# Tables' rows by partition, own semaphores and four buffers for the h rows, and a division moved to ScalarE, in a graph network on one Trainium2 core

## What is computed

```
L0: h = relu(x@W1 + b1) @ W2;  out = segment_sum(h[src]*norm, dst) + own term + b2
L1: out = gcn(relu(gcn(x, W1)), W2), gcn(h) = segment_sum(norm*h[src], dst) + own term
L2: z = leaky_relu(x) @ W;  e = leaky_relu(el[src] + er[dst]);  ex = exp(e - emax[dst])
    out = segment_sum(ex/denom[dst] * z[src], dst) + bias
L3: messages = relu([x[src], x[dst], edge] @ mW1 + mb1) @ mW2
    out = relu([x, segment_sum(messages, dst)] @ uW1 + ub1) @ uW2 + ub2
```

## Time and profile before

| | |
|---|---|
| median of 3 runs | 2941.12 us (2938.37 to 2942.83) |
| the profiled execution | 2938.16 us |
| its span, first to last instruction | 2936.4 us |
| busy share of the span: PE, DVE, ACT, POOL | 74%, 68%, 49%, 74% |
| mean granted TensorE clock | 0.848 of full speed |
| DMA packets | 624033, of them 536606 under 512 B; 338.13 MB |
| chain that ended last, by engine | POOL 57%, issue 19%, PE 9%, DVE 8%, DMA 3% |

### The profile page before, as it was taken

One profiled execution on the slowest core, in us unless ns is written; L12 is line 12 of the kernel. 1 busy time (PEld: TensorE's weight loads), 2 busy tenths in 40 slices (PEclk: granted clock), 3 DMA queues, 4 the chain that ended last, 5 costly groups with the idle time before them and its releaser, 6 DMA issues.

```text
span 2936.4 us, 39046 instructions
## 1 busy us (share of the span) xinstructions
PE 2171.1 (74%) x10332; PEld 1155.7 (39%) x10332; DVE 1984.6 (68%) x3848; ACT 1429.8 (49%) x2755; POOL 2169.0 (74%) x1666
## 2 busy tenths in 40 slices
PE   3998899968778757777687759998356576666665
PEld 1444444434445324444343434444155233333332
DVE  6665688858888747777599968998699343333332
ACT  2877677745444436665344437777222232223332
POOL 7888878778888268886788858888233688888887
PEclk9999999979898768888789979999555787777777
DMA  7998522224556455555344445555477322222221
GB/s 210 285 271 241 144 57 54 59 58 93 129 130 141 93 128 125 128 133 125 78 112 113 111 95 127 141 137 125 94 191 186 77 62 52 55 57 57 54 53 26
DMA packets 624033, 338.13 MB, mean 115 GB/s; under 512 B 536606, under 2 KB 585100, under 8 KB 623817
## 3 DMA queue, kind: packets, MB, share of 16 engines
q1 hardware_dynamic: 550217, 288.96, 39.1%
q0 software_dynamic: 73600, 46.68, 9.4%
HBM read 203.61 MB, written 130.80 MB: 114 GB/s over the span
## 4 chain that ended last, share of the span: by engine, by line
POOL 57%; issue 19%; PE 9%; DVE 8%; DMA 3%; SPq 1%; ACT 1%; DVEq 0%; POOLq 0%; ACTq 0%
POOL g_row L857 42%; POOL x_with_info L864 8%; POOL out_rows L864 8%; PE bank L1075 2%; PE bank L1098 1%; DVE rT L1685 1%; PE bank L984 1%; PE pair L1055 1%; DMA g_row<-t_x,gidx 1%; PE pair L984 1%; DMA g_row<-in_x,dst_i 1%; DVE x_r L1662 1%; DVE ss L1608 1%; PE pair L1066 0%; DVE w_r L2007 0%
## 5 line engine op out<-in xcount | busy, mean ns | idle before, releaser
L857 POOL DMA_INDIRECT g_row<-t_x,gidx x600 | 808.1, 1347 | 258.6 <-issue 217.3
L1281 ACT ACTIVATE hid<-pair,b_up 128x1000 f32<-128x1000 f32 x375 | 406.0, 1083 | 42.9 <-PE pair L1056 42.1
L1076 PE MATMUL bank<-hid,w_dn 128*64 128x500 f32 x750 | 420.8, 644 | 0.0
L1075 PE MATMUL bank<-hid,w_dn 128*64 128x500 f32 x750 | 420.7, 644 | 0.0
L1055 PE MATMUL pair<-xT,w_top 64*128 64x500 f32 x550 | 316.7, 657 | 15.5 <-ACT hid L1281 15.0
L857 POOL DMA_INDIRECT g_row<-x_with_info,src_i x200 | 275.3, 1377 | 63.8 <-issue 55.8
L1056 PE MATMUL pair<-xT,w_bot 64*128 64x500 f32 x550 | 317.5, 658 | 0.0
L857 POOL DMA_INDIRECT g_row<-t_h,gidx x200 | 261.5, 1307 | 75.7 <-issue 75.7
L857 POOL DMA_INDIRECT g_row<-in_x,dst_i x200 | 261.1, 1306 | 68.7 <-issue 68.1
L1262 ACT ACTIVATE xT<-bank 128x500 f32<-128x500 f32 x275 | 160.2, 583 | 295.3 <-DVE rT L1685 163.2
L864 POOL DMA_INDIRECT out_rows<-n_r,fidx x200 | 248.8, 1244 | 61.6 <-issue 60.3
(11 more groups left out here) (257 smaller groups left out, 5205.0 us busy)
## 6 DMA issues: line engine op xcount, KB each, us to landing
x_in<-in_x_cols SPq DMA_DIRECT2D x100, 250.0 KB
x_with_info<-wide SPq DMA_DIRECT2D x50, 476.0 KB
wide<-in_x SPq DMA_DIRECT2D x50, 448.0 KB
out_rows<-x_r SPq DMA_DIRECT2D x100, 224.0 KB
l_k<-keep_row SPq DMA_DIRECT2D x150, 125.0 KB
l_a<-t_x SPq DMA_DIRECT2D x150, 112.0 KB
l_k<-on_row SPq DMA_DIRECT2D x50, 250.0 KB
t_x<-x_r SPq DMA_DIRECT2D x100, 112.0 KB
```

The source lines that it names most:

```text
L857: return g.indirect_dma_start(out=to, out_offset=None, in_=table, in_offset=bass.IndirectOffsetOnAxis(ap=index[:, tile:tile + 1], axis=0), ...
L1075: T.matmul(run.down[0:D, 0:CH], w_dn[a.stage][:, 0:D], hid[a.b2][:, 0, :], start=True, stop=True)
L1076: T.matmul(run.down[D:128, 0:CH], w_dn[a.stage][:, 0:D], hid[a.b2][:, 1, :], start=True, stop=True)\
L1281: A.activation(hid[a.b2][:, :, :], run.up[a.b2][:, :, 0:CH], ACT.Relu, bias=b_up[:, a.stage:a.stage + 1]).then_inc(Cn["hid"], 1)
```

## The change

The rows of a table are stored by partition: chunk c, partition p, tile k is row c*500 + p*4 + k; iso block b, partition p, place j is row b*1000 + p*8 + j. The two iotas behind `gidx` follow. `in_pairs` is gone, and stores of iso rows go out in two pieces of 2 KB runs. The h2 rows get four buffers (two idle ones of the same size are taken in) and four semaphores of their own; the x2 stores get three. In G, v_r is made on ScalarE by four activations with the reciprocal as scale, at the head of ScalarE's slot; DVE's reciprocal waits for the v_r before. The diff, cut:

```diff
         def chunks(ap):
-            return ap.rearrange("(c k p) f -> c p k f", k=TC, p=R)
+            return ap.rearrange("(c p k) f -> c p k f", k=TC, p=R)
+
+        def chunk_pairs(ap):
+            return ap.rearrange("(b s p k) f -> b p s (k f)", s=2, k=TC, p=R)

         def blocks(ap):
-            return ap.rearrange("(b j p) f -> b p j f", j=TB, p=R)
+            return ap.rearrange("(b p j) f -> b p (j f)", j=TB, p=R)
...
-        h2_r = [b[0:R, :] for b in h2_r_all]
+        h2_r = [b[0:R, :] for b in h0_r_all + h2_r_all]
...
-                        for to, frm in in_pairs(blocks(t1_d[E:2 * E, :])[a.b], x1_r[a.r4]):
+                        for to, frm in in_two(blocks(t1_d[E:2 * E, :])[a.b], x1_r[a.r4][:, :]):
...
-                        for to, frm in in_pairs(blocks(t2_d[E:2 * E, :])[a.b], h2_r[a.b % 2]):
-                            sp.dma_start(to, frm).then_inc(s1_sem[a.b % 2], 16)
+                        for to, frm in in_two(blocks(t2_d[E:2 * E, :])[a.b], h2_r[a.b % 4][:, :]):
+                            sp.dma_start(to, frm).then_inc(h2_sem[a.b % 4], 16)
                         sp.wait_ge(Cn["rows"], normed(a))
-                        for to, frm in in_pairs(blocks(t3_d[E:2 * E, :])[a.b], x2_r[a.r3]):
-                            sp.dma_start(to, frm).then_inc(s1_sem[a.b % 2], 16)
+                        for to, frm in in_two(blocks(t3_d[E:2 * E, :])[a.b], x2_r[a.r3][:, :]):
+                            sp.dma_start(to, frm).then_inc(s1_sem[a.b % 3], 16)
...
-                for to, frm in in_two(blocks(t1_d[0:E, :])[b], n_view(a_rows[b % 2])):
+                for to, frm in in_two(chunk_pairs(t1_d[0:E, :])[b], a_rows[b % 2].rearrange("p (s c) -> p s c", s=2)):
...
-                        for to, frm in in_two(blocks(t4_d[E:2 * E, :])[b], n_view(third_out[b % 2])):
+                        for to, frm in in_two(blocks(t4_d[E:2 * E, :])[b], third_out[b % 2]):
...
-            g.iota(slot_id[:, :], pattern=[[R, NT]], base=1, channel_multiplier=1,
+            g.iota(slot_id[:, :], pattern=[[CH, NC], [1, TC]], base=1, channel_multiplier=TC,
...
-            g.iota(gbase[:, :], pattern=[[R, NT]], base=E, channel_multiplier=1,
+            g.iota(gbase[:, :], pattern=[[BLK, NI], [1, 2], [2, TC]], base=E, channel_multiplier=TB,
...
@@ ScalarE, slot_g @@
+                if c := at(2):
+                    k, q, h, p = c
+                    at_least(act, LE["rden"], k + 1)
+                    at_least(act, LE["t2"], k)
+                    for i in range(TC):
+                        part = A.activation(v_r[:, i * D:(i + 1) * D], AT[0:R, i * 128:i * 128 + D], ACT.Copy,
+                                            scale=lrden[:, i:i + 1])
+                    part.then_inc(LE["t1"].sem, 1)
...
-                        at_least(dve, iso_sem1[a.b % 2], 128 * (a.b // 2))
-                        V.tensor_tensor(h2_r[a.b % 2][:, :], run.rows[a.b2][0:R, :], x1_r[a.r4][:, :], ALU.subtract).then_inc(Cn["h2"], 1)
+                        at_least(dve, Cn[f"h2st{a.b % 4}"], 32 * (a.b // 4))
+                        V.tensor_tensor(h2_r[a.b % 4][:, :], run.rows[a.b2][0:R, :], x1_r[a.r4][:, :], ALU.subtract).then_inc(Cn["h2"], 1)
...
-                            par, times = iso_stored(a.s - 3)
-                            dve.wait_ge(iso_sem1[par], 128 * times)
+                            dve.wait_ge(iso_sem1[SEQ[a.s - 3].b % 3], 32 * (SEQ[a.s - 3].b // 3 + 1))
...
@@ DVE, slot_g @@
                     at_least(dve, LE["den"], k + 1)
+                    at_least(dve, LE["t1"], k)
                     V.reciprocal(lrden[:, :], lden[:, :]).then_inc(LE["rden"].sem, 1)
-                if c := at(2):
-                    k, q, h, p = c
-                    at_least(dve, LE["rden"], k + 1)
-                    at_least(dve, LE["t2"], k)
-                    V.tensor_tensor(v4(v_r[:, :]), AT65[:, :, 0:D], spread(lrden[:, :], TC), ALU.mult).then_inc(LE["t1"].sem, 1)
```

More of the change, by code:

```diff
@@ L310, in build @@
         Cn = sems("chain", "rowsT xT up hid dn res resT h2 h2b sq ssum std rstd"
-                           " rows y sq2 ssum2 std2 rstd2 rows2 info in0 in1 in2 out0 out1 dsq0 dsq1 dsq2 dsq3 scaled based base0 base1 s0st0 s0st1 s1st0 s1st1")
+                           " rows y sq2 ssum2 std2 rstd2 rows2 info in0 in1 in2 out0 out1 dsq0 dsq1 dsq2 dsq3 scaled based base0 base1 s0st0 s0st1 s1st0 s1st1 s1st2 h2st0 h2st1 h2st2 h2st3")
         ctx.enter_context(nc.allow_non_contiguous_dma(reason="bias columns and the chunks' neighbours, once"))
@@ L446, in third_steps @@
                     yield step, (k - at) // 2
[L448 to L452, removed]
         def in_two(to, frm):
@@ L601, in _ @@
             base_sem = [Cn["base0"], Cn["base1"]]
-            s0_sem, s1_sem = [Cn["s0st0"], Cn["s0st1"]], [Cn["s1st0"], Cn["s1st1"]]
+            s0_sem, s1_sem = [Cn["s0st0"], Cn["s0st1"]], [Cn[f"s1st{r}"] for r in range(3)]
+            h2_sem = [Cn[f"h2st{r}"] for r in range(4)]
             asked = [0]
@@ L632, in slot @@
                         sp.wait_ge(Cn["based"], a.b + 1)
-                        for to, frm in in_two(blocks(base0_d)[a.b], n_view(own_base[a.b % 2][:, :])):
+                        for to, frm in in_two(blocks(base0_d)[a.b], own_base[a.b % 2][:, :]):
                             sp.dma_start(to, frm).then_inc(base_sem[a.b % 2], 16)
@@ L664, in ld_a @@
                 at_least(sp, LA["t2"], b - 3)
-                for to, frm in in_two(n_view(a_base[b % 4]), blocks(base0_d)[b]):
+                for to, frm in in_two(a_base[b % 4], blocks(base0_d)[b]):
                     sp.dma_start(to, frm).then_inc(A_ld[b % 4].sem, 16)
@@ L739, in ld_third @@
             def ld_third(b):
-                for to, frm in in_two(n_view(third_in[b % 2]), blocks(t3_d[E:2 * E, :])[b]):
+                for to, frm in in_two(third_in[b % 2], blocks(t3_d[E:2 * E, :])[b]):
                     sp.dma_start(to, frm).then_inc(third_ld[b % 2], 16)
@@ L745, in third @@
                 if k < 0:
+                    for r in range(3):
+                        sp.wait_ge(s1_sem[r], 32 * len(range(r, NI, 3)))
                     for b in range(2):
-                        sp.wait_ge(s1_sem[b], 128 * len(range(b, NI, 2)))
                         ld_third(b)
@@ L928, in _ @@
             for r in range(2):
-                pool.wait_ge([Cn["s0st0"], Cn["s0st1"]][r], 64 * len(range(r, NI, 2)))
+                pool.wait_ge([Cn["s0st0"], Cn["s0st1"]][r], 32 * len(range(r, NI, 2)))
             all_stored(pool, A_st, NI)
             gather_level(t1_d, B_ga, LB["msg"])
-            for r in range(2):
-                pool.wait_ge([Cn["s1st0"], Cn["s1st1"]][r], 128 * len(range(r, NI, 2)))
+            for r in range(4):
+                pool.wait_ge(Cn[f"h2st{r}"], 32 * len(range(r, NI, 4)))
             all_stored(pool, B_st)
@@ L1595, in _ @@
             assert c[1] == PREP_ALL
-            iso_sem0, iso_sem1 = [Cn["s0st0"], Cn["s0st1"]], [Cn["s1st0"], Cn["s1st1"]]
+            iso_sem0, iso_sem1 = [Cn["s0st0"], Cn["s0st1"]], [Cn[f"s1st{r}"] for r in range(3)]
             def chain(run):
@@ L1609, in first @@
                     if a and a.stage == 0 and a.iso:
-                        at_least(dve, iso_sem0[a.b % 2], 64 * (a.b // 2))
+                        at_least(dve, iso_sem0[a.b % 2], 32 * (a.b // 2))
                         V.tensor_copy(info_r[:, a.b * TB:(a.b + 1) * TB, :], xs_rows[a.b % 4][:, :, D:XW]).then_inc(Cn["info"], 1)
                     if a and a.stage == 1 and a.iso:
-                        at_least(dve, iso_sem1[a.b % 2], 128 * (a.b // 2))
-                        V.tensor_tensor(h2_r[a.b % 2][:, :], run.rows[a.b2][0:R, :], x1_r[a.r4][:, :], ALU.subtract).then_inc(Cn["h2"], 1)
+                        at_least(dve, Cn[f"h2st{a.b % 4}"], 32 * (a.b // 4))
+                        V.tensor_tensor(h2_r[a.b % 4][:, :], run.rows[a.b2][0:R, :], x1_r[a.r4][:, :], ALU.subtract).then_inc(Cn["h2"], 1)
                         dve.wait_ge(Cn["h2"], a.b + 1)
-                        V.tensor_tensor(n_view(h2_r[a.b % 2][:, :]), n_view(h2_r[a.b % 2][:, :]), row_bias(1, TB),
+                        V.tensor_tensor(n_view(h2_r[a.b % 4][:, :]), n_view(h2_r[a.b % 4][:, :]), row_bias(1, TB),
                                         ALU.subtract).then_inc(Cn["h2b"], 1)
@@ L1653, in rest @@
                                 par, times = iso_stored(a.s - 4)
-                                dve.wait_ge(iso_sem0[par], 64 * times)
+                                dve.wait_ge(iso_sem0[par], 32 * times)
                         if a.stage == 1 and a.s >= 3 and SEQ[a.s - 3].iso:
-                            par, times = iso_stored(a.s - 3)
-                            dve.wait_ge(iso_sem1[par], 128 * times)
+                            dve.wait_ge(iso_sem1[SEQ[a.s - 3].b % 3], 32 * (SEQ[a.s - 3].b // 3 + 1))
                         if a.stage == 2:
@@ L1914, in _ @@
             for r in range(2):
```

(7 more changed lines are left out.)

## The result

The changed kernel took **2922.79 us** at the median of four runs (2918.18 to 2927.77); the kernel before, run beside it on the same chip, 2940.21 us (2938.37 to 2942.83). The ratio is 0.994 with a 95% interval of 0.9922 to 0.9959: faster by 0.6%. I had predicted 2943.6 us with a range of 2926 to 2959, and no change that can be told as the likeliest.

The account below looks back on a forecast made before the run. It took GpSimd's gathers and scatters as the bound in all stages but G, plus the waits between stages, and the AT loop in G. Sum -15.8 - 2.2 + 20.5 = +2.5 us on 2941.12: 2943.6 us, range 2926 to 2959.

Parts of the forecast that it names:

- no change that can be told: Whole kernel: the forecast itself, a time of 2935 to 2947 us; chance 0.42.
- Point 1: Tail of A: four h buffers and separate semaphores remove DVE's waits before the h row; 15.8 us gained.
- the two waits: Tail of A: DVE idle 8.59 and 8.15 us before the h row, 16.7 us, of which 15.8 stay won.
- The rivals in which the wait passes over to the x2 store, whole or for one turn: Tail of A: whole, 2959 us, chance 0.03; one turn, +8 us, 2951 us, chance 0.10.
- Point 2: Stage ends: fewer, longer store pieces shorten landings by 0.6 and 1.0 us, 0.6 for B, C, G; 2.2 us gained.
- Point 4: G: v_r as four ScalarE activations, 1.02 us, lengthens the AT loop's turn from 3.28 to 3.85 us; 20.5 us lost.
- The DVE rival: G: DVE is the bound, so moving v_r off it gains 17 us; 2906 us, chance 0.07.
- Point 3: Row order, iotas and loads in 256-byte runs: nothing on a path, GpSimd's gathers keep 1.27 us; no effect.

Follow-up runs that it names:

- buffers alone: Kernel before with only the four h buffers and separate semaphores; old row order, four-piece stores, v_r on DVE: 2923.43 us, ratio 0.9929.
- rows alone: Kernel before with only rows by partition and two-piece stores; two h buffers on shared semaphores, v_r on DVE: 2919.11 us, ratio 0.9924.
- v_r alone: Kernel before with only v_r moved from DVE to four ScalarE activations in G: 2955.91 us, ratio 1.0044.

## Why the prediction was wrong

**Point 1, the wait in A: right.** I took 15.8 us for the two waits; buffers alone take 14.2 to 15.0 from the gap. The x2 store did not come into the way, as I had argued from its landing. The rivals in which the wait passes over to the x2 store, whole or for one turn, are out.

**Point 2, the landings: about right in sum, too dear in each landing.** A's last store takes 2.80 us and not 2.85, where I expected 0.6 less; it is 2.85 to 2.96 us in the five profiles of the old order and 2.69 to 3.02 in the eight of the new one. The last store of the third pass takes 2.51 and not 2.99, where I expected 1.0 less; 2.89 to 3.02 us in the old order, 2.48 to 2.66 in the seven of the new one whose chain passes through it. The gaps gave 1 to 2 us in A (rows alone) and 1.8 at the mean from D to G: 3 to 4 us against 2.2. By the Trainium skill (DMA: Bandwidth & Descriptors, "Why small descriptors are slow (HBM only)") it would have been 27% of a landing at most; the two landings shrank by 2% and 16%, which stays below that bound.

**Point 4, v_r in G: right in its mechanism, a little too dear.** Four activations take 0.93 us, not 1.02: a turn is 3.76 us against my 3.85, and 49 turns of 0.09 us are the 4.5 us by which the sum was too high. I expected +20.5 us; the profiles show +16.0, and the comparisons of times +13 (v_r alone) and +16 to +20 (the change with and without it). The DVE rival, G faster by 17 us, is out while AT has one bank; with two, DVE is the nearest bound, and taking v_r off it shortens G by 7 us. The rule of the Trainium skill (ScalarE: Activation LUTs, "Rules for kernel authors") that multiplications belong on VectorE held for the kernel as changed; with two banks G was shorter by 7 us against the rule, in one profile of each, while the times overlap. By the same page ("What ACT_TABLE_LOAD costs") one activation would take 332 ns and four, overlapping, 1.05 us, an estimate from its fixed costs and its price per element; the trace has 315 ns for one (L1409, median) and 0.93 us for four, which is less.

**Point 3, the row order: this is the step that failed.** I wrote of the other order of rows "nothing on a path; GpSimd's gathers keep their 1.27 us", and that M stays as long as before. The median did stay. The mean did not: GpSimd's busy time in M fell by 11.2 us and M by 10.5, in all six profiles with the new order and M's code untouched, and in none with the old. What the runs show in its place is the meeting of GpSimd's transfers with DVE's scan over the messages: in the new order fewer transfers start early in it. With M at -10.5 in place of nothing, G at +16.0 and the rest as measured, the sum is -18.4 - 1.8 + 16.0 - 10.5 = -14.7 us; the medians say -17.4 and -18.8. Without M it would be -4.2 us, 2937 us, inside my range. My mistake had two parts. I read the cost of a transfer from its median, though the same row showed a longest of 2461 ns and M's busy time (512.93 us of 397 transfers, 1.29 each, half of them scatters of some 1.2 us and half gathers of 1.27) held the rest. And I took the time inside M to be GpSimd's alone, so that no other engine could move it, where what DVE does at the moment a transfer starts moves its length between 1.2 and 2.2 us. So I had no case, and no width in the range, for a stage that the change touches only by its addresses.

The rows part also gave more in the comparison of times (23 us) than the 14 us that the four places of its profile add up to. How much of that is the spread of four runs is open. So is how the new addresses bring the scan to another place between the transfers: the waits of M differ a little, and no run took the order of the stores apart from that of the gathers. That it came out as a gain is luck: nothing in the change aims at it, and two small copies on ScalarE take a third of it back.

## What to carry to other kernels

A stage bound by one engine's many equal instructions is priced by the sum of their durations, not by the median: the difference between the two is what other engines can give or take, and any change of timing elsewhere, even of addresses, can move it. A handover of a single buffer between two engines is a loop: what is moved onto it lengthens every turn, whatever it takes off the busier engine. A second buffer changes which place is the better one: here it took 27 us off G with v_r on ScalarE and 3 us with v_r on DVE. Test the parts of a mixed change each alone: here one of three cost 13 to 20 us of the 38 us that the others won together, and the change without it (2904.0 us), or with it and a second bank (2898.5 us), beats both kernels.

## What was not expected of the hardware

GpSimd's indirect transfers take longer when they start during a DVE scan whose two operands are tiles in SBUF: 2.14 us and not 1.27 in the case shown, up to 2.23 us in the thirteen profiles, with the end some 1.0 to 1.1 us after the scan's end. During a scan of the same length that reads PSUM (and works on the other partitions) they keep their 1.2 to 1.3 us. In M of the kernel before, 48 of the 400 transfers start in the first kind and take 18.6 us more than their usual 1.27 or 1.20 us.

The coupling works the other way also. In G DVE's scan takes 1545 ns at the mean before and 1251 after, for the same shape. Before, 40 of 49 scans start while GpSimd's multiplication runs, and take 1.61 us at the mean, the other nine 1.24; after, 4 of 49 do, and the other 45 take 1.23. It is the move of v_r that does this: with v_r alone it is 5 of 49, and in the change with v_r back on DVE 42.

```profile
L1996 DVE TENSOR_TENSOR_SCAN agg<-l_k,agg,wide 65x500 f32<-65x500 f32 x49 | 75.7, 1545 | 1.6 <-POOL wide L948 1.5
```

```profile
L2001 DVE TENSOR_TENSOR_SCAN agg<-l_k,agg,wide 65x500 f32<-65x500 f32 x49 | 61.3, 1251 | 2.1 <-POOL wide L947 1.9 <-issue 0.2
```

So of the longer turn that v_r on ScalarE costs, DVE got 14 us back in shorter scans, and could do nothing with them, since it waits for TensorE 0.93 us a turn at the mean. Nearly halving the number of packets (624033 to 337483) took 0.05 us and 0.48 us from the two landings on the path.
